# Padding the causal keys on VectorE from rows of a whole head group, and turning the running maxima round on ScalarE, in a four-stage hybrid transformer layer

## The reference

```python
# stage a: 32 score heads of width 4, 16 value heads of width 8
att = einsum('bhtd,bhsd->bhts', q * hd ** -0.5, k) / sqrt(hd)
att = softmax(where(causal, att, -inf))             # T = 1024
att = att[:, :, 0] - lambda_full * att[:, :, 1]     # pairs of heads
out = rms_normalised(att @ v) * gamma * (1 - LAMBDA_INIT); return out @ w_proj
# stage b: for every token, H = 16 heads of C = 64 scalars
scores = Q[..., :, None] * K[..., None, :]          # masked: key index <= query index
attn = softmax(scores) @ V; return attn @ Wo + bo
```

## Time and profile before

| | |
|---|---|
| median of 3 runs | 2318.2 us (2314.12 to 2320.08) |
| the profiled execution | 2317.3 us |
| its span, first to last instruction | 2315.6 us |
| busy: PE, DVE, ACT, POOL | 1877.9, 1890.4, 1045.0, 1444.3 us |
| granted TensorE clock, mean | 0.931 of full speed |

### The profile page before, as it was taken

One profiled execution on the slowest core, in us unless ns is written; L12 is line 12 of the kernel. 1 busy time (PEld: TensorE's weight loads), 2 busy tenths in 40 slices (PEclk: granted clock), 3 DMA queues, 4 the chain that ended last, 5 costly groups with the idle time before them and its releaser, 6 DMA issues. The chain is left out here.

```text
span 2315.6 us, 35954 instructions
## 1 busy us (share of the span) xinstructions
PE 1877.9 (81%) x14226; PEld 1394.4 (60%) x14226; DVE 1890.4 (82%) x1551; ACT 1045.0 (45%) x1408; POOL 1444.3 (62%) x673
## 2 busy tenths in 40 slices
PE   2291799999985678988888889889889888898886
PEld 1140344444434467777777777778777777777785
DVE  6370577777745499999999999999999999999984
ACT  1050466666671135444444444444444444535440
POOL 8120122222220188897987987988978979879871
PEclk9695899999996589999999999999999999999996
DMA  2011000000000000000000000000000000000000
GB/s 79 16 25 26 8 7 8 9 7 7 7 1 0 0 1 1 1 1 2 1 1 1 1 1 1 1 1 1 1 1 1 1 1 1 1 1 1 1 1 18
DMA packets 10618, 14.24 MB, mean 6 GB/s; under 512 B 4416, under 2 KB 7392, under 8 KB 10336
## 3 DMA queue, kind: packets, MB, share of 16 engines
q1 hardware_dynamic: 8928, 11.33, 1.8%
q10 hardware_dynamic: 1536, 0.61, 0.1%
HBM read 4.57 MB, written 1.05 MB: 2 GB/s over the span
## 5 line engine op out<-in xcount | busy, mean ns | idle before, releaser
L1042 POOL TENSOR_TENSOR b_p_ring<-b_p_ring,b_m 128x2048 f32<-128x2048 f32 (+7 forms) x384 | 1250.9, 3293 | 207.4 <-DVE b_p_ring L951 206.1
L1074 ACT ACTIVATE b_p_ring<-b_p_ring 128x2048 f32<-128x2048 f32 (+7 forms) x384 | 535.7, 1412 | 777.1 <-POOL b_p_ring L1042 775.5
L1134 PE MATMUL b_ps<-k_ident,b_ev_ring 128*128 128x128 f32 (+6 forms) x4608 | 596.3, 281 | 148.2 <-DVE b_ev_ring L1000 144.4
L1000 DVE TENSOR_TENSOR b_ev_ring<-b_p_ring,b_ps 128x2048 f32<-128x2048 f32 (+7 forms) x384 | 633.2, 1653 | 3.1 <-PE b_ps L1100 1.6
L1134 PEld LDWEIGHTS b_ps<-k_ident,b_ev_ring 128*128 128x128 f32 (+6 forms) x4608 | 503.8, 138 | 217.9 <-DVE b_ev_ring L1000 192.9
L951 DVE TENSOR_TENSOR b_p_ring<-b_ps,b_key 128x2048 f32<-128x2048 f32 (+7 forms) x384 | 633.4, 1657 | 0.0
L1134 PE MATMUL b_ps<-k_ident,b_p_ring 128*128 128x128 f32 (+6 forms) x4608 | 579.2, 277 | 15.6 <-ACT b_p_ring L1074 9.5
L1134 PEld LDWEIGHTS b_ps<-k_ident,b_p_ring 128*128 128x128 f32 (+6 forms) x4608 | 514.4, 137 | 24.4 <-ACT b_p_ring L1074 10.2
L562 DVE TENSOR_REDUCE a_negm<-a_ps 128x1 f32<-128x768 f32 (+7 forms) x384 | 350.4, 953 | 192.7 <-PE a_ps L451 188.5
L545 ACT ACTIVATE a_ex<-a_ps 128x512 f32<-128x512 f32 (+3 forms) x768 | 333.1, 498 | 300.0 <-PE a_ps L490 291.7
L361 POOL TENSOR_SCALAR_AFFINE_SELECT a_ex<-a_ex 128x512 f32<-128x512 f32 x128 | 81.3, 635 | 439.0 <-ACT a_ex L545 437.5
(11 more groups left out here) (157 smaller groups left out, 1037.1 us busy)
## 6 DMA issues: line engine op xcount, KB each, us to landing
rk<-rows_k SPq DMA_DIRECT2D x384, 8.0 KB
rq<-rows_q SPq DMA_DIRECT2D x192, 16.0 KB
k_wqkv<-in_wqkv SPq DMA_DIRECT2D x1, 2048.0 KB, 8.4
out<-x_all SPq DMA_DIRECT2D x4, 256.0 KB, 2.4
k_wo<-in_wo SPq DMA_DIRECT2D x1, 512.0 KB, 9.2
k_w_attn<-in_w_attn ACTq DMA_DIRECT2D x1, 192.0 KB, 2.5
k_reset_max<-in_reset_max ACTq DMA_DIRECT2D x1, 128.0 KB, 4.8
k_reset_min<-in_reset_min SPq DMA_DIRECT2D x1, 128.0 KB, 9.0
```

The lines of the kernel that those rows point to most:

```text
L1000: nc.vector.tensor_tensor(chunk(ev_ring, c), chunk(p_ring, c), over_queries(values(c), c), ALU.mult).then_inc(ev_done.sem, 1)
L1042: nc.gpsimd.tensor_tensor(pc, pc, over_rows(m[:, half].rearrange("p i h -> p (i h)"), c), ALU.subtract).then_inc(shifted.sem, 1)
L1074: nc.scalar.activation(pc, pc, ACT.Exp).then_inc(exp_done.sem, 1)
L1134: last = nc.tensor.matmul(ps[0:width, bank, b // IB * P:(b // IB + 1) * P], rows[:, r, b:hi].rearrange("p i h -> p (i h)"), k["ident"][:], ...
```

## The change

Rows are now spread by head group. In `rq` and the new tile `rk_of_group` (two slots), term t of the six takes 16 partitions, 4 for each of the four heads, so one transfer of 16 partitions per term moves what took four; the maxima's rows begin at partition 96. DVE makes the four padded tiles of `rk` by multiplying `rk_of_group` with a column of 0 and 1 per head (`head_rows`, loaded with the constants). `parts` has three steps instead of five: ACT writes the first bfloat16 part from PSUM itself, and the second subtraction writes the third part. SP issues the rows of jobs 0 and 1 at the end of its list in the first block. POOL fills only `rk_of_group[96:]` with ones, DVE clears only `rq[96:]`, and the `ps_n` product with the power and copy that belong to it moves ahead of the pieces. In phase b ACT copies `kmax` and `kmin` into `kmaxr` and `kminr` in the order in which `maxima` needs them.

```diff
+GROUP_ROWS = 4 * A_HD
+M_ROW = len(TERM_Q) * GROUP_ROWS
...
+def spread_keys(sp, rk_of_group, rows_k, spread, n):
+    g, b = n // BATCH, n % BATCH
+    for t, part in enumerate(TERM_K):
+        sp.dma_start(rk_of_group[t * GROUP_ROWS:(t + 1) * GROUP_ROWS, n % 2],
+                     rows_k[g * GROUP_ROWS:(g + 1) * GROUP_ROWS, part, b * T:(b + 1) * T]).then_inc(spread, 16)
...
             sp.wait_ge(loaded.sem, 16 * len(rest))
+            for b in range(BATCH):
+                done = 3 * (b + 1) * S // BATCH
+                sp.wait_ge(first_part.sem, 2 * (b + 1) * S // BATCH)
+                sp.wait_ge(q_step.sem, done)
+                spread_queries(sp, rq, rows_q, queries_spread[0], 0, b, b + 1)
+                sp.wait_ge(k_step.sem, done)
+                spread_keys(sp, rk_of_group, rows_k, keys_spread[b], b)
...
-            nc.gpsimd.memset(rk[:], 0.0).then_inc(filled.sem, 1)
+            nc.gpsimd.memset(rk_of_group[M_ROW:], 1.0).then_inc(filled.sem, 1)
...
+                nc.scalar.activation(rows_q[:, 0, cols(s)], ps_qk[:, s % 2, 0], ACT.Copy, scale=1.0 / A_HD).then_inc(first_part.sem, 1)
...
             for g in range(1, GROUPS):
-                spread_queries(g)
-            for n in range(3, JOBS):
-                spread_keys(n)
+                spread_queries(sp, rq, rows_q, queries_spread[g], g, 0, BATCH)
+            for n in range(2, JOBS):
+                sp.wait_ge(padded.sem, padded.at(n - 2, 4))
+                spread_keys(sp, rk_of_group, rows_k, keys_spread[n % 2], n)
...
                 if u == 0:
-                    pe.wait_ge(keys_spread[n % 3], SPREAD * (n // 3 + 1))
+                    pe.wait_ge(padded.sem, padded.at(n, 4))
...
+            def pad(n, hh):
+                if hh == 0:
+                    dve.wait_ge(keys_spread[n % 2], SPREAD * (n // 2 + 1))
+                    if n >= 3:
+                        dve.wait_ge(exp_done.sem, exp_done.at(n - 3, STEPS))
+                nc.vector.tensor_scalar(rk[:, n % 3, hh, :], rk_of_group[:, n % 2, :], k["head_rows"][:, hh:hh + 1], None,
+                                        ALU.mult).then_inc(padded.sem, 1)
...
+            for hh in range(4):
+                pad(0, hh)
             for n in range(-1, JOBS):
-                for kind, job, u in items(n):
+                for i, (kind, job, u) in enumerate(items(n)):
                     item(kind, job, u)
+                    if 0 <= i - PAD_ITEM < 4 and n + 2 < JOBS:
+                        pad(n + 2, i - PAD_ITEM)
...
-                dve.wait_ge(scan_done.sem, scan_done.at(it, 4))
+                dve.wait_ge(turned_back.sem, turned_back.at(it, 2))
...
-                nc.vector.tensor_tensor(m[:, half], q, at(kmax), ALU.mult).then_inc(m_step.sem, 1)
+                nc.vector.tensor_tensor(m[:, half], q, at(kmaxr), ALU.mult).then_inc(m_step.sem, 1)
...
+            def turn_back(it):
+                act.wait_ge(scan_done.sem, scan_done.at(it, 4))
+                for straight, back in ((kmax, kmaxr), (kmin, kminr)):
+                    nc.scalar.copy(back[:], straight[:].rearrange("p (h c) -> p c h", h=H)[:, ::-1, :]).then_inc(turned_back.sem, 1)
...
+                    if not last and c == TURN_BACK_AT:
+                        turn_back(it + 1)
...
+            turn_back(0)
```

More of the change, by code:

```diff
@@ L121, in _ @@
             sp.wait_ge(loaded.sem, 16 * len(rest))
+            for b in range(BATCH):
[5 more added lines that the diff above has]
+                spread_keys(sp, rk_of_group, rows_k, keys_spread[b], b)
         def parts(eng_ns, eng, step, rows, i, s):
             left = qk[:, i, cols(s)]
[L126 to L132, removed]
+            first, second, third = (rows[:, part, cols(s)] for part in range(3))
+            eng.wait_ge(first_part.sem, 2 * s + i + 1)
+            eng_ns.tensor_tensor(left, left, first, ALU.subtract).then_inc(step.sem, 1)
+            eng.wait_ge(step.sem, step.next(0))
+            eng_ns.tensor_copy(second, left).then_inc(step.sem, 1)
+            eng.wait_ge(step.sem, step.next(0))
+            eng_ns.tensor_tensor(third, left, second, ALU.subtract).then_inc(step.sem, 1)
+            step.next(0)
         @block.vector
@@ L154, in _ @@
             dve.wait_ge(const_step.sem, const_step.next(0))
+            dve.wait_ge(norm_psum.sem, 1)
+            nc.vector.tensor_copy(t32[:, 1, :], ps_n[:]).then_inc(const_step.sem, 1)
+            dve.wait_ge(const_step.sem, const_step.next(0))
             for s in range(S):
@@ L239, in _ @@
             turn(0)
+            pe.wait_ge(filled.sem, 3)
+            pe.wait_ge(const_step.sem, 4)
+            nc.tensor.matmul(ps_n[:], k["ones32"][:], t32[:, 0, :], start=True, stop=True).then_inc(norm_psum.sem, 1)
             for s in range(S):
@@ L874, in phase_b @@
         kmin = sb("kmin", [P, HID])
+        kmaxr = sb("kmaxr", [P, C, H])
+        kminr = sb("kminr", [P, C, H])
         m = sb("m", [P, 2, FIRST, H])
@@ L1224, in build @@
         rq = sb_a("rq", [P, GROUPS, BATCH, T], BF16)
+        rk_of_group = sb_a("rk_of_group", [P, 2, T], BF16)
         rk = sb_a("rk", [P, 3, 4, T], BF16)
@@ L1275 @@
     arrays["mask_t"] = (NEG * later.T).astype(bf)
+    head_rows = np.zeros((P, 4), np.float32)
+    for h in range(4):
+        for t in range(len(TERM_Q)):
+            head_rows[t * GROUP_ROWS + h * A_HD:t * GROUP_ROWS + (h + 1) * A_HD, h] = 1.0
+        head_rows[[M_ROW + 4 * part + h for part in range(3)], h] = 1.0
+    arrays["head_rows"] = head_rows
     arrays["rank4"] = rows(np.arange(E, 0, -1).astype(np.float32))
```

79 lines of the change are left out of this document (29 added, 50 removed).

## The result

The changed kernel took 2243.8 us (median of 4 runs, 2239.2 to 2247.2) against 2317.8 for the kernel before, run beside it (4 runs, 2314.1 to 2320.1): a ratio of 0.968, 95% interval 0.966 to 0.971. It is 74 us faster; the prediction was 2246. The profiled execution took 2247.2 us, its span is 2245.5, so 70.1 us less than the span before. The four runs of the change lie in two pairs, 2239.2 and 2240.5 us (granted clock 0.943 and 0.944) and 2247.1 and 2247.2 us (0.937), and the profiled one is of the second.

The account below looks back on a forecast made before the run. It took the start, one hole (both from SP's serial transfers) and PE's speed to bound the first attention, DVE the second. Attention −100.3 and phase b +28.9 made −71.4: 2317.3 to 2246 us, range 2207 to 2270.

Parts of the forecast that it names:

- The start: First block and head of phase a2: PE begins attention at 53.3 us instead of 94.8, −41.5 us.
- Rival 3: DVE's pads cost 1.22 us each, by a surcharge or by POOL, giving 2295 us; chance 0.10.
- The hole: Attention: PE's wait for keys 3, queued behind 168 transfers on SP, goes; −66.1 us.
- The pads, +5.6: DVE's four pads per job in jobs 2 to 15 cost 0.4 us a job, 14 × 0.4 = +5.6 us.
- Job 1's pads: Job 1's pads on DVE, where it reduces almost without a break: +1.7 us.
- Maxima straight, −24.3: Phase b: 64 DVE instructions read the extrema in order, saving 0.379 us each, −24.3 us.
- Turning back, +49.5 and +3.7: Phase b: ACT's copies of 1.8 us make DVE wait 3.3 us in 15 tiles, +49.5; first tile's copies +3.7.
- rival 2: Phase b: DVE's wait at half 0's finish only replaces the next half's 3.24 us, giving 2196 us; chance 0.08.
- The page against the row: ACT's strided copy in phase b: 1.8 us with DVE's surcharge, against a page formula's 1.04 us (total about 2221).

Follow-up runs that it names:

- spread_late: The changed kernel, but with all spreading transfers of jobs 0 and 1 issued at the head of phase a2 instead of in the first block: 2250.5 us, ratio 0.971.
- split_with_step: The changed kernel, but POOL writes the three parts of the negated maxima with a step of 64 bytes, as before the change: 2253.4 us, ratio 0.973.
- no_turning: The changed kernel without ACT's copies and their waits; DVE reads kmax and kmin in order, so in the wrong column order: 2184.4 us, ratio 0.942.
- turning_alone: The kernel before, with only phase b taken from the changed kernel: 2349.3 us, ratio 1.015.

## Why the prediction was right, and where it was not exact

*The start.* Right in its order, 2.6 us short: PE at 55.9, not 53.3. The first query piece was evicted at 28.6 (28.0), SP began at 36.7 (36.0), the block ended at 52.5 (51.4); the transfers cost what was said. The larger part, 1.4 us, is the price of the pads: 3.15 us for the first four where 4 × 0.43 stood. The row taken was nearly right for pads that run alone, 0.48 us each in every later job; at the head two of the four are slowed while POOL works, and `spread_late` shows 1.67 for four behind POOL's work. Rival 3 had named such a surcharge, but for all jobs.

*The hole.* As reckoned, gone whole. Keys 2 were in time, and no wait for a DMA took its place.

*The pads, +5.6.* Here a step failed, though a small one. The sum took the middle between nothing and 0.8 us; `split_with_step` shows 0.07 us a job. Job 1's pads cost 2.0 where 1.7 stood: the first addition comes 27.9 us behind PE's begin (83.80 − 55.87), 26.0 before. But a term was missing: the new layout of the rows of the maxima shortens POOL's casts from 322 to 211 ns, and as DVE waits for POOL there, 0.38 us a job came off. The prediction had costed only the transfers' side of the layout. Together −4 us where +5.6 stood, and with the start and job 1 the attention gave −107.6, not −100.3.

*Maxima straight, −24.3.* Right: (0.381 + 0.361) × 32 = 23.7 by the rows, and 24.3 by `no_turning` (20.7 to 24.7 by its trace).

*Turning back, +49.5 and +3.7.* The mechanism was right in every link: ACT stops for 6 us in front of the copies, the inversion is behind them, DVE waits in 15 tiles for half 0, and half 1's wait stays (rival 2 is out). The size was off by the copy: 2.0 us, not 1.8, which made the wait 3.56 us instead of 3.3. The waits grew by 107.9 − 54.4 = 53.5, the first tile's is 3.9, and 2.6 us more of waiting stands before the products with the values (5.7 us for 3.1). With the −23.7 that is 36.3 of the 37.2 measured.

*The page against the row.* The copy took 2.0 us in steps and 1.05 in order. The Trainium skill's "Advanced Engine Details and Errata", SBUF Cachelines, says that a different line per access costs something, and excepts no engine. This trace agrees: 0.96 us more for 1024 elements on ACT, and 0.38 for 512 on DVE. The formula of the Trainium skill's "ScalarE: Activation LUTs", What ACT_TABLE_LOAD costs, gives an estimate of 1.04 us. It holds for the straight copy (1.05) and is half of the one in steps. Had the prediction taken the surcharge of DVE's row as a proportion (1.065 / 0.686) a copy would have been 1.65; as an amount per element it gave 1.8. ACT's own amount is 0.94 ns per element where DVE's is 0.74.

The total, 2246 against 2243.8, is nearer than its terms, and that is luck: 7 us too little gain in the attention and 8 us too little loss in phase b (5 like for like, by the trace of `turning_alone`) cancelled.

## What to carry to other kernels

Work moved to an engine that is half idle is not free: ask what stands behind it in that engine's list. Here 4 us of copies in the wrong place cost 3.6 a tile, and two chunks further, behind the work that another engine waits for, nearly nothing. Where an engine in order waits (ACT's 102 us in front of the copies), first look for something behind the wait that could go ahead of it. And a slack is not a rate: the first four pads cost 0.07 us a job and the next four 1.97.

## What the runs showed of the hardware

A step on ACT's access costs the same on the read (256 bytes) as on the write (64 bytes): 2.01 us for 1024 float32 either way, 1.05 in order. POOL's cast of 32 elements falls from 322 to 211 ns when its 2-byte results lie in fours rather than 64 bytes apart. A bfloat16 multiplication of 128 x 1024 on DVE by a scalar per partition takes 0.48 us. Four of them take 1.67 us while POOL rests, and 3.15 in the change, where POOL fills from 52.53 to 53.48 and scales from 53.55 to 56.62. Not all four are slowed:

```profile
52.57 1.19 DVE L573 TENSOR_SCALAR rk<-rk_of_group,k_head_rows 128x1024 bf16<-128x1024 bf16 x1 [5.67 <-PEq L99]
```
```profile
53.69 1.25 DVE L573 TENSOR_SCALAR rk<-rk_of_group,k_head_rows 128x1024 bf16<-128x1024 bf16 x1
```
```profile
54.85 0.87 DVE L573 TENSOR_SCALAR rk<-rk_of_group,k_head_rows 128x1024 bf16<-128x1024 bf16 x2
```

The first two take 1.2 us, the last two 0.47 each although POOL's scaling is still going on, and this scaling took 3.07 us here and 2.78 with DVE at rest (in `spread_late` and before). So POOL's work costs DVE something in some places and nothing in others, and an average (0.79) hides that. What decides it was not tried. The Trainium skill's "GPSIMD Engine Reference", Key points, says that the two engines share their way into SBUF and collide on some forms of DVE's instructions. The first two rows agree with that without proving it; the third shows that beside a running POOL instruction there need be no delay.
